# A graph layer on one core: additions first in the loop, a maximum on VectorE, and the last two groups in another order

## The reference

```
h = max(layernorm(x), 0)
msg_in   = [h[src], h[dst], edge features]      # 64 + 64 + 32 per edge
messages = silu(msg_in @ W1 + b1) @ W2 + b2
logits   = silu(msg_in @ Wa1 + ba1) @ Wa2 + ba2
att      = softmax(logits over all edges)
agg      = segment_sum(messages * att, dst)
out      = x + silu([h, agg] @ Wu1 + bu1) @ Wu2 + bu2
```

## Time and profile before

| | |
|---|---|
| median of 3 runs | 2541.52 us |
| the profiled execution's own time | 2545.81 us |
| its span, first to last instruction | 2544.0 us |
| busy: POOL, PE matmul, PE load | 60%, 52%, 44% |
| busy: DVE, ACT | 37%, 36% |
| mean granted TensorE clock | 0.653 |
| DMA | 228.42 MB, 90 GB/s on average |

### The profile page before, as it was taken

One profiled execution on the slowest core, in us unless ns is written; L12 is line 12 of the kernel. 1 busy time (PEld: TensorE's weight loads), 2 busy tenths in 40 slices (PEclk: granted clock), 3 DMA queues, 4 the chain that ended last, 5 costly groups with the idle time before them and its releaser, 6 DMA issues.

```text
span 2544.0 us, 20784 instructions
## 1 busy us (share of the span) xinstructions
PE 1335.2 (52%) x7010; PEld 1126.5 (44%) x7010; DVE 953.6 (37%) x1722; ACT 925.1 (36%) x1106; POOL 1529.6 (60%) x1628
## 2 busy tenths in 40 slices
PE   5245555555455555555455555555555455555556
PEld 3234444444444444444444444444444444444444
DVE  4234334433333333433333333333333333443345
ACT  3333333433333333343333333343333333333333
POOL 3665656666666656666666666666666665666650
PEclk8666666666766666666766666666766666666667
DMA  7433333333333333333333333333333333333321
GB/s 193 105 88 84 88 85 91 87 88 92 97 88 87 87 85 90 88 88 89 98 90 88 87 86 89 89 87 87 97 93 88 88 87 85 91 87 87 95 67 27
DMA packets 101988, 228.42 MB, mean 90 GB/s; under 512 B 45185, under 2 KB 65461, under 8 KB 91637
## 3 DMA queue, kind: packets, MB, share of 16 engines
q1 hardware_dynamic: 47588, 120.63, 18.2%
q0 software_dynamic: 51584, 105.75, 16.3%
q10 hardware_dynamic: 2704, 0.66, 0.1%
HBM read 218.91 MB, written 8.00 MB: 89 GB/s over the span
## 4 chain that ended last, share of the span: by engine, by line
another core or an unknown queue 53%; ACT 17%; DVE 14%; issue 11%; PE 3%; DVEq 1%; ACTq 0%; SPq 0%; DMA 0%
ACT s L516 5%; DVE bank L897 5%; ACT L516 4%; ACT comb L484 3%; DVE prod L884 3%; ACT comb L490 3%; DVE lg L886 3%; PE bank L624 1%; ACT bank L504 1%; PE bank L613 1%; DVE lgb L944 1%; PE bank L575 1%; DVE gmax L904 1%; ACT fade L506 1%
## 5 line engine op out<-in xcount | busy, mean ns | idle before, releaser
L396 POOL DMA_INDIRECT p_rows<-p_tab,src_all x1612 | 1521.6, 944 | 943.7 <-issue 466.9
L613 PE MATMUL bank<-q_win,comb 128*128 128x128 f32 x3224 | 825.6, 385 | 842.6 <-issue 832.1
L613 PEld LDWEIGHTS bank<-q_win,comb 128*128 128x128 f32 x3224 | 669.0, 279 | 952.2 <-issue 950.9
L516 ACT ACTIVATE s<-bank 128x512 f32<-128x512 f32 x403 | 239.0, 594 | 1434.4 <-DVE bank L897 1424.7
L874 DVE SCALAR_TENSOR_TENSOR acc<-acc,fade,bank 65x96 f32 x80 | 24.8, 310 | 1330.3 <-remote 1326.7
L624 PE MATMUL bank<-hot,v 128*65 128x96 f32 x3224 | 393.7, 300 | 165.2 <-issue 149.7
L624 PEld LDWEIGHTS bank<-hot,v 128*65 128x65 f32 x3224 | 378.4, 180 | 186.0 <-issue 169.0
L897 DVE TENSOR_TENSOR bank<-bank,p_rows 128x512 f32<-128x512 f32 x403 | 277.0, 688 | 15.7 <-issue 15.7
L484 ACT ACTIVATE comb<-dst_b,row_of 96x1024 f32<-96x1024 int32 (+1 forms) x162 | 217.8, 1345 | 55.3 <-DMA dst_b<-dst_row 55.3
L490 ACT ACTIVATE comb<-comb,ones 96x1024 f32<-96x1024 f32 (+1 forms) x162 | 218.8, 1351 | 2.7
L861 DVE TENSOR_TENSOR hot<-bank,rel 128x960 f32<-128x960 f32 x162 | 185.1, 1143 | 0.0
(11 more groups left out here) (107 smaller groups left out, 321.0 us busy)
## 6 DMA issues: line engine op xcount, KB each, us to landing
dst_b<-dst_row SPq DMA_DIRECT2D x80, 960.0 KB
p_rows<-p_tab,src_all POOLq DMA_INDIRECT x1612
comb<-efT SPq DMA_DIRECT2D x80, 320.0 KB
q_win<-q_tab SPq DMA_DIRECT2D x81, 48.0 KB
p_tab<-s SPq DMA_DIRECT2D x12, 256.0 KB
q_tab<-s SPq DMA_DIRECT2D x12, 256.0 KB
out<-s SPq DMA_DIRECT2D x6, 256.0 KB, 2.3
x_sb<-x SPq DMA_DIRECT2D x2, 512.0 KB, 5.0
```

What stands on the lines that cost most here:

```text
L396: pool.indirect_dma_start(p_rows[:, a, t * H2:(t + 1) * H2], None, p_tab, bass.IndirectOffsetOnAxis(src_all[:, g * TG + t:g * TG + t + 1], ...
L516: nc.scalar.activation(silu_rows(a, q), halves(ps_z[q][:]), ACT.Silu).then_inc(silu_ok, 1)
L613: last = nc.tensor.matmul(ps_z[q][:, (t % TQ) * H2:(t % TQ + 1) * H2], comb[:, a, t * P:(t + 1) * P], q_win[:, a, :], start=True, stop=True)
```

## The change

- In `group` on DVE the additions of group g stand first: quarters 0, 1, 2 with the rest of group g-1 (logits, bias, maximum) between them, then the first logits of g, quarters 3 and 4, and only then `add_part`, now of group g-2, the one-hot matrices and the weighted rows of g-1.
- The addition of quarter 3 is in two parts: 128 columns, signalled by `tile_ok`, and 384 columns, signalled by `z_ok`. POOL waits for `tile_ok` in front of the quarter's first gather and for `z_ok` in front of its second.
- The maximum over the partitions is taken on DVE alone: the bias is added four times, three of them moving 32 partitions down beside the first 32; then a reduction over 32 partitions, a 32x32 transpose, a reduction, and four small writes of `neg_max`. `column_max` and `spread_max` leave the loop on PE.
- The last two groups have an order of their own: two node indices are read ahead, the last `sums` waits for each half of its one-hot matrix by itself, an Exp on a constant stands ahead of ACT's last weights, and the final `acc` addition stands behind DVE's branch.
- `own_part` has banks for six blocks and reuses one for the seventh; five of the seven products are issued before the last `sums`.

```diff
@@ POOL
-                    if not (isinstance(g, int) and g < 2):
-                        pool.wait_ge(z_ok, (g - 2) * NQ + q + 1)
+                    if g > 1:
+                        if q == 3:
+                            pool.wait_ge(tile_ok, g - 1)
+                        else:
+                            pool.wait_ge(z_ok, (g - 2) * NQ + q + 1)
                     for t in range(q * TQ, (q + 1) * TQ):
+                        if g > 1 and t == 3 * TQ + 1:
+                            pool.wait_ge(z_ok, (g - 2) * NQ + q + 1)
@@ ACT
-                act.wait_ge(negm_ok, g + 1)
+                act.wait_ge(negm_ok, 4 * (g + 1))
...
+            nc.scalar.activation(rz[:], ones[:, 0:1], ACT.Exp)
             weights(LAST, 0)
@@ PE
-                if late:
-                    column_max(g - 1)
                 for q in [q for q in (0,) if q in quarters]:
                     zmm(nxt, 1 - a, q)
-                if late:
-                    spread_max(g - 1)
...
             own_part(0)
             own_part(1)
-            column_max(LAST)
-            spread_max(LAST)
-            pe.wait_ge(zp_ok, 1)
             pe.wait_ge(silu_ok, LAST * NQ + TL // TQ)
-            nc.tensor.matmul(ps_zall, ones[:], zp[:], start=True, stop=True).then_inc(zall_done, 1)
-            sums(LAST)
+            for b in range(2, 5):
+                own_part(b)
+            pe.wait_ge(acc_ok, LAST)
+            pe.wait_ge(v_ok, NG)
+            for t in range(TL):
+                if t in (0, TL // 2):
+                    pe.wait_ge(hot_ok, 2 * LAST + 1 + 2 * t // TL)
...
-            own_part(2)
+            own_part(5)
             for b in range(UB + 1):
                 aggregate(b)
-                if 3 + b <= UB:
-                    own_part(3 + b)
+                if b == 1:
+                    own_part(6)
@@ DVE, add_rows
+                n = 0
+                if q == 3:
+                    n = H2
+                    nc.vector.tensor_tensor(ps_z[q][:, 0:n], ps_z[q][:, 0:n], p_rows[:, a, q * 512:q * 512 + n], ALU.add).then_inc(tile_ok, 1)
+                nc.vector.tensor_tensor(ps_z[q][:, n:], ps_z[q][:, n:], p_rows[:, a, q * 512 + n:(q + 1) * 512], ALU.add).then_inc(z_ok, 1)
@@ DVE, the maximum
+            def biased(g):
+                T = tiles(g)
+                dve.wait_ge(s_ok, (g + 1) * 4)
+                nc.vector.tensor_scalar(lgb[:, 0:T], lg[:, 0:T], ba2c[:], None, ALU.add).then_inc(lg_ok, 1)
+                for k in range(1, 4):
+                    lanes = slice(32 * k, 32 * (k + 1))
+                    nc.vector.tensor_scalar(lgb[0:32, k * T:(k + 1) * T], lg[lanes, 0:T], ba2c[lanes, :], None, ALU.add).then_inc(lg_ok, 1)
+            def lane_max(g):
+                nc.vector.tensor_reduce(qmax[:], lgb[0:32, 0:4 * T], AX.X, ALU.max).then_inc(qmax_ok, 1)
+            def spread_max(g):
+                nc.vector.transpose(qmaxB[:], qmax[:].broadcast_to([32, 32])).then_inc(qmaxB_ok, 1)
+                nc.vector.tensor_reduce(top[:], qmaxB[:], AX.X, ALU.max).then_inc(top_ok, 1)
@@ DVE, group
+                late = g > 0
+                add_rows(g, a, 0)
+                if late:
+                    logits(1 - a, 2, NQ, silu_ok, g * NQ, s_ok, g * 4 - 2)
+                add_rows(g, a, 1)
+                if late:
+                    biased(g - 1)
+                add_rows(g, a, 2)
+                if late:
+                    lane_max(g - 1)
+                    spread_max(g - 1)
+                    running_max(g - 1)
+                logits(a, 0, 2, silu_ok, g * NQ + 2, s_ok, g * 4)
+                if g < LAST - 1:
+                    add_rows(g, a, 3)
+                    add_rows(g, a, 4)
+                if g > 1:
+                    add_part(g - 2, a)
+                if late:
+                    one_hots(g - 1, 0)
+                    one_hots(g - 1, 1)
+                    weighted(g - 1, 1 - a)
```

More of the change, by code:

```diff
@@ L622, in sums @@
                 T = tiles(g)
+                if g == 1:
+                    pe.wait_ge(bad_ok, 1)
+                    nc.tensor.transpose(ps_part[0:1, P:2 * P], bad[:, 2:3], ident[:])
                 for t in range(T):
@@ L625, in sums @@
                 last.then_inc(part_done, 1)
-            def column_max(g):
-                pe.wait_ge(pmax_ok, g + 1)
-                if g == 1:
-                    pe.wait_ge(bad_ok, 1)
-                    nc.tensor.transpose(ps_small[0:1, P:2 * P], bad[:, 2:3], ident[:])
-                nc.tensor.transpose(ps_small[0:1, 0:P], pmax[:], ident[:]).then_inc(maxT_done, 1)
-            def spread_max(g):
-                pe.wait_ge(gmax_ok, g + 1)
-                nc.tensor.matmul(ps_small[:, 0:1], ones[0:1, :], gmax[:], start=True, stop=True).then_inc(maxB_done, 1)
             def group(g, a):
@@ L658, in own_part @@
                 n = (units(b) + 1) // 2 * P
-                wait(pe, su_ok, b - 4)
-                nc.tensor.matmul(ps_u[b % 5][0:rows_of(b), 0:n], wu1d[:, 0:rows_of(b)], hP[:, b * UT // 2 * P:b * UT // 2 * P + n], start=True, stop=False)
+                wait(pe, su_ok, b - 5)
+                nc.tensor.matmul(ps_u[b][0:rows_of(b), 0:n], wu1d[:, 0:rows_of(b)], hP[:, b * UT // 2 * P:b * UT // 2 * P + n], start=True, stop=False)
             for q in range(NQ):
@@ L666, in _ @@
             own_part(1)
-            column_max(LAST)
-            spread_max(LAST)
-            pe.wait_ge(zp_ok, 1)
             pe.wait_ge(silu_ok, LAST * NQ + TL // TQ)
-            nc.tensor.matmul(ps_zall, ones[:], zp[:], start=True, stop=True).then_inc(zall_done, 1)
-            sums(LAST)
+            for b in range(2, 5):
[5 more added lines that the diff above has]
+                    pe.wait_ge(hot_ok, 2 * LAST + 1 + 2 * t // TL)
+                if t == TL // 2 + 2:
+                    pe.wait_ge(zp_ok, 1)
+                    nc.tensor.matmul(ps_zall, ones[:], zp[:], start=True, stop=True).then_inc(zall_done, 1)
+                last = nc.tensor.matmul(ps_part[0:U1, 0:WIN], v[:, t, :], hot[:, t * WIN:(t + 1) * WIN], start=(t == 0), stop=(t == TL - 1))
+            last.then_inc(part_done, 1)
             pe.wait_ge(flag_ok, 1)
@@ new lines, in running_max @@
+            def running_max(g):
+                dve.wait_ge(top_ok, g + 1)
+                wait(dve, negm_ok, 4 * g)
+                for k in range(4):
+                    nm = neg_max[32 * k:32 * (k + 1), bass.ds(g, 1)]
+                    if g == 0:
+                        nc.vector.tensor_scalar(nm, top[:], -1.0, None, ALU.mult).then_inc(negm_ok, 1)
+                    else:
+                        nc.vector.scalar_tensor_tensor(nm, top[:], -1.0, neg_max[0:32, bass.ds(g - 1, 1)], ALU.mult, ALU.min).then_inc(negm_ok, 1)
@@ L923, in group @@
             def group(g, a):
-                nxt = following(g)[0]
-                late = not (isinstance(g, int) and g == 0)
-                T = tiles(g)
-                for q in range(T // TQ):
-                    if q + 1 < T // TQ:
-                        add_rows(g, a, q + 1)
-                    if q == 2 and late:
-                        one_hots(g - 1, 1)
-                    if q == 1:
-                        logits(a, 0, 2, silu_ok, g * NQ + 2, s_ok, g * 4)
-                    if q == T // TQ - 1:
-                        logits(a, 2, T // TQ, silu_ok, g * NQ + T // TQ, s_ok, g * 4 + 2)
-                    if q == 0 and late:
-                        group_max(g - 1)
-                    if q == 1 and late:
-                        running_max(g - 1)
-                        one_hots(g - 1, 0)
-                    if q == 2 and late:
-                        weighted(g - 1, 1 - a)
```

108 lines of the change are left out of this document (52 added, 56 removed).

## The result

| | before | after |
|---|---|---|
| median of 4 runs | 2541.55 us | 2485.01 us (2480.22 to 2488.36) |
| the profiled execution's own time | 2545.81 us | 2483.66 us |
| its span | 2544.0 us | 2482.0 us |
| first gather issued | 45.97 | 39.95 |
| POOL's stops over 1 us, sum | 79, 439.8 us | 78, 366.4 us |

The ratio is 0.9779, with the interval 0.9764 to 0.9794: 56.5 us faster. The forecast of 2469 us was 16 us too low; its own range (2455 to 2497) holds the result.

The account below looks back on a forecast made before the run. A closed loop of waits bounds the kernel: POOL on DVE, DVE on PE's signal, held until gathers are worked off. 2545.8 - 81 + 8 + 0.5 = 2473 us profiled, median 4.3 lower: 2469 us, range 2455 to 2497.

Parts of the forecast that it names:

- The held signal and the circle: POOL waits for DVE, DVE for PE's signal, held until POOL's gathers are worked off, 3.97 us behind the last.
- The 2135 us: Whole kernel at 24.96 us per group, if gathers did not hold PE's signal and POOL set the pace.
- What is "worked off": Gathers issued since POOL's last stop, said to be worked off at 1.43 us each before PE's signal reaches others.
- -81 us for the shorter way: DVE's start to POOL's gather falls to 0.58 us, saving 1.04 us at each of 78 stops; bounds -72 to -90.
- +8 us for PE's shortage: PE may lack matmul records for quarter 3 when the signal comes: 0.1 us per group, from 0 to 90 us.
- 0 for the maximum on DVE: About 1.4 us more DVE work per group, hidden in time DVE spends waiting; 110 us if not covered.
- rival D: Three more copy-like bias additions on DVE hold POOL's gathers 0.24 us each: +58 us, 2527 us; chance 0.03.
- The 384 columns beside a gather: The rest of quarter 3's addition on DVE runs beside a 0.94 us gather, at no cost.
- +0.5 us for the end: From last gather to end: maximum 8 us later, -3.7 to the rescaling, -4 in the output phase; bounds -5 to +8.
- The own products that leave the output phase: Three products (2.08 us for one) leave a PE that DVE waits for: -4 us, bounds 0 to -6.
- Rival "POOL's own pace": The 1.43 us per gather limits only the closed loop, so POOL's issue pace gives 2135 us; chance 0.03.
- A: Quarter 3's product is seen before POOL runs out, so releases hardly stop POOL: 28.6 us per group, 2416 us; chance 0.14.

Follow-up runs that it names:

- experiment 8: Changed kernel with the maximum over partitions on PE and DVE as before: three runs 2666.76 to 2681.04 us, one 2587.54 us, no ratio given.
- experiment 9: Changed kernel with every second gather left out from group 2 on (10 instead of 20 per group): 1362.32 us, ratio to before 0.5397.
- 2 and 3: Changed kernel with the last 4 tiles of `sums` left out in all groups but the last, 2106.32 us; with two more products ahead of `sums`, 2107.16 us.
- experiment 4: Changed kernel with the maximum's new DVE instructions issued a second time on scratch tiles: 2110.18 us, ratio to before 1.0002.
- experiment 5: Changed kernel again without any edit, beside the kernel before on chip 13: 2451.96 us, ratio 0.9712.
- experiment 6: Changed kernel with own products 2 to 6 issued where the kernel before has them, on chip 13: 2449.55 us, ratio to before 0.97.
- experiments 7 and 10: Changed kernel with quarter 3's addition in one piece, 2471.76 us; changed kernel with quarter 3's product ahead of `sums`, 2481.76 us; both on chip 2.
- experiment 1: Changed kernel with quarter 3's addition in one piece of 512 columns, on chip 6: 2105.28 us, ratio to before 0.999.

## Why the prediction was right, and where it was off

*The held signal and the circle.* Right, on the chips of its kind. In the profile after, 20 gathers stand between stops, released by the 128-column addition; `add_part` waits no more. The signal comes 3.80 us behind the last gather in the stop shown, 3.97 us in the forecast. Experiment 8 shows the hold with PE idle, experiment 9 that the long cycle goes with the gathers. What the prediction left out of its sum is that PE too is slow beside the gathers, though it saw one such pause (at 1038.33). It also gave the matmul counts of its stretches in the wrong order: 79 belong to 16 gathers and 80 to 20, which doesn't touch the argument. The Trainium skill, "SBUF — State Buffer", section "Who interferes with whom", has the rule that a DMA never contends with a compute engine. The 2135 us that the prediction worked out by it are near the 2106 and 2108 us of chips 5 and 6, and wrong on the others.

*What is "worked off".* Only the number of 1.43 us per gather stands; the reading is doubtful. In the changed kernel's first profile POOL's last gather ends at 1048.39 and DVE starts at 1052.19. The DMA engines' traffic from 1047 to 1050 us, and from 1050 to 1052, is

```profile
DMA packets 69, 0.13 MB, mean 44 GB/s; under 512 B 37, under 2 KB 37, under 8 KB 69
...
DMA packets 0, 0.00 MB, mean 0 GB/s; under 512 B 0, under 2 KB 0, under 8 KB 0
```

The rows had been moved 2 us before the signal was seen. What holds it is open, and so is why two chips of four in the experiments don't have it. Since each was used in one session, it isn't even shown that the chip makes the difference.

*-81 us for the shorter way.* Right. DVE's way is 0.57 us (forecast 0.58) and the stops that PE doesn't end are 4.46 us, 5.51 us before: 1.05 us each (forecast 1.04).

*+8 us for PE's shortage.* Right in kind, but sized at half: 34 stops x 0.47 us = 16 us. How often PE is named depends on the chip, 8 times on chip 13; that it is a shortage of records was argued from the counts, and the experiments for it (2 and 3) had no stops to act on. That all stops together came to -73.4 us, the forecast's -73, is luck in part: 74 x -1.05 and +16 are -62 us, and the rest is one stop fewer (5.5 us) and shorter stops at the start (6.1 us).

*0 for the maximum on DVE.* Right; experiment 4 shows it on a chip without stops only. The gathers beside its bias additions take 0.94 or 0.95 us in the profile after, so rival D falls. What the prediction did not see is that the rest loses without this edit, as far as experiment 8 goes.

*The 384 columns beside a gather.* Costed at nothing, and that step failed by its second wait on POOL. The columns themselves are done in time (1022.97 + 0.56, the gather is issued at 1024.97), but 19 second gathers pause for 0.40 us more: 7.6 of the 7.9 us of short pauses. The profiles with POOL's second wait at its stop and all gathers have 19 of them each (after, experiments 5, 6 and 8); experiments 7 and 10, without that wait at the stop, have none. Why it is every fourth stop is open.

*+0.5 us for the end.* This step failed most: +9.2 us, beyond its bound of +8. The later maximum (+8) and the shorter way to the rescaling (-5, forecast -3.7) were sized well. The own products that leave the output phase were given -4 us, and the phase grew by 6. Two things were missed. First, only two large products leave it, 80 records against 84: before, product 2 stood ahead of the rescaling, while PE waited for DVE's branch, and now product 5 stands behind PE's own branch and ahead of the first aggregate. That path is 2.7 us longer and gives back half of what DVE's shorter way had won. Second, the products had been priced by their own duration, at a clock that stays as it is. With them in their place the clock rises within the phase, without them it stays at the lower level to the end (experiment 6 shows that part). Where it falls differs too: before, it was at the lower level from 2505 us on, 13 us ahead of the rescaling; after, it was at the upper one until 2450.8, while PE stood idle for 3.3 us behind `sums` (2448.2 to 2451.5). Why it rises when it does is open.

So the 16 us between forecast and median are 8.7 of the end and 7.9 of the short pauses. On chip 13 the gain was 70 us, near the forecast's 72, but not by the forecast's sum: the short pauses (478.3 us) and the output phase (32.1 us) are as long there, and only the stops are shorter (333.7 us in all).

*The chances.* Rival "POOL's own pace" had 0.03 as a form of A. It was no outcome of the change: on two chips both kernels take about that time, and for them "no change" would have been right.

## What to carry to other kernels

When a wait is put down to nothing that the profile can name, and its length follows the work of an engine that the waiting one doesn't need, suspect that the signal is late and not the work, and test it where the engine that signals is idle (experiment 8); then shorten what stands between its arrival and the engine that it stops, and move what you can ahead of the held point. Take the profile on a second chip before tuning such a wait: here it is worth 2.2 to 2.9% on some and nothing on others. Work taken off an engine in a short last phase is to be priced with the clock that it leaves behind, not only with its own duration. When one engine's branch is hidden, look whether another engine's branch now ends the wait.

## What was not expected of the hardware

- The same program takes 2107.93 and 2106.22 us on two chips and 2522.13, 2527.84 and 2541.55 us in the other three measurements; the first two are 16 to 17% less, and each has a spread under 0.7%. TensorE's clock doesn't explain it: the mean granted TensorE clock is 0.68 in the faster profile of experiment 1, 0.66 in that of experiment 5.
- A signal of PE reached DVE 16.0 us late while POOL issued gathers, and the next one within 0.04 us of the product's end once POOL was silent (experiment 8).
- Beside the gathers PE itself does one record every 1.4 to 2.2 us where it otherwise takes 0.23 us (after, 1033.54 to 1050.53). On chip 6 its longest wait for "issue" is 3.1 us and stands behind the loop (experiment 1).
- Within an idle time of PE of 3.3 us TensorE's clock fell to its lower level (1.2 GHz) and stayed there for the last 31 us, though PE was busy for 27 us of them (the output phase after).
- A second wait ahead of a second gather costs 0.40 us in 19 stops of 78, the same number in four profiles, on chips 13 and 2 and in the first pair.
